# Gates from PSUM, spill experts behind the places, turned parts from ScalarE: one change to a two-layer attention and expert kernel

## What is computed

```python
# block 1: cross attention to ctx, 16 heads of 8
x = x + attention(ln(x), ctx, ctx) @ Wo.T + bo
# block 2: 8 experts of 128, two per token, and a shared one
logits = h @ gate_w.T                       # gate0
idx = top_k(logits + lb_bias, 2)
w = sigmoid(logits[idx]); w = w / (sum(w) + 1e-6)
x = x + sum_e w_e * (relu(h @ w1[e].T)**2 @ w2[e].T) + shared
# block 3: causal self attention (q1, k1, v1), norm, attention to ctx (k2, q2), norm,
#          c + relu(c @ Wf + bf), norm
# block 4: router (gate1), the first of the softmax's top two, 7 routed experts of 512, a shared one
probs = softmax(h @ w_router); top = argmax(probs)
x = x + 2 * probs[top] * (silu(h @ w_gate[top]) * (h @ w_up[top])) @ w_down[top] + shared
```

## Time and profile before

| | us |
|---|---|
| median of 3 runs | 356.95 (356.26 to 357.55) |
| the profiled execution | 356.45 |
| its span, first to last instruction | 354.4 |
| TensorE busy in it | 283.8 |
| VectorE busy | 279.7 |
| ScalarE busy | 205.7 |
| GpSimd busy | 156.7 |

### The profile page before, as it was taken

The page is one execution under the profiler, slowest core; times in us unless marked ns, Lnnn a source line. Parts: engine busy times, 40 slices in busy tenths (PEclk is TensorE's granted clock), DMA queues, the critical chain, the costliest instruction groups (busy, mean ns, idle before and its releaser), DMA issues.

```text
span 354.4 us, 8691 instructions
## 1 busy us (share of the span) xinstructions
PE 283.8 (80%) x3349; PEld 210.3 (59%) x3349; DVE 279.7 (79%) x726; ACT 205.7 (58%) x431; POOL 156.7 (44%) x157
## 2 busy tenths in 40 slices
PE   0396864549999977999997988574797999979994
PEld 0154653424566733787775866433564799758993
DVE  4889999796745589689899557878779998897732
ACT  1464873334757444898886689431873558735561
POOL 9904669653653030344544334411431567442541
PEclk9999995556999989999999899766679999999999
DMA  8502022432020000000000000000003102040030
GB/s 249 227 1 91 13 79 91 130 138 91 15 112 0 0 2 1 3 2 2 4 2 1 2 3 2 2 0 0 2 2 139 42 2 93 2 178 2 18 107 30
DMA packets 6592, 16.62 MB, mean 47 GB/s; under 512 B 660, under 2 KB 2968, under 8 KB 6552
## 3 DMA queue, kind: packets, MB, share of 16 engines
q1 hardware_dynamic: 6552, 16.08, 12.9%
HBM read 10.83 MB, written 0.52 MB: 32 GB/s over the span
## 4 chain that ended last, share of the span: by engine, by line
PE 42%; DVE 34%; ACT 9%; POOL 7%; issue 7%; POOLq 0%; DVEq 0%; ACTq 0%
DVE MX L1337 6%; PE ps L985 5%; PE ps L776 5%; PE ps L777 5%; PE ps L778 5%; DVE prl L636 4%; PE ps L837 2%; ACT pr L1117 2%; DVE stat L1292 2%; ACT prh L1121 2%; ACT lnx L1163 2%; DVE pr L1518 2%; PE ps L973 2%; PE ps L909 1%; PE ps L825 1%
## 5 line engine op out<-in xcount | busy, mean ns | idle before, releaser
L636 POOL TENSOR_TENSOR prl<-pr,prh 128x384 f16<-128x384 f32 (+1 forms) x48 | 49.9, 1042 | 73.9 <-ACT prh L1121 73.9
L1117 ACT ACTIVATE pr<-ps 128x384 f32<-128x384 f32 (+1 forms) x96 | 51.7, 538 | 21.9 <-DVE prl L636 8.9
L1337 DVE TENSOR_REDUCE MX<-ps 128x8 f32<-128x512 f32 (+2 forms) x80 | 52.0, 681 | 8.5 <-PE ps L861 4.1
L1121 ACT ACTIVATE prh<-ps 128x384 f16<-128x384 f32 (+1 forms) x96 | 51.7, 538 | 0.3 <-PE ps L778 0.2
L642 POOL TENSOR_TENSOR prl<-pr,prh 128x512 f16<-128x512 f32 x28 | 33.5, 1205 | 41.1 <-ACT prh L1156 41.1
L745 POOL TENSOR_TENSOR wl<-wraw,wh 128x512 f16<-128x512 f32 (+1 forms) x30 | 35.2, 1198 | 29.3 <-DVE wh L1221 29.2
L636 DVE TENSOR_TENSOR prl<-pr,prh 128x384 f16<-128x384 f32 (+1 forms) x48 | 33.4, 695 | 8.0 <-ACT prh L1121 7.8
L1156 ACT CAST prh<-pr 128x512 f16<-128x512 f32 x28 | 17.2, 618 | 15.0 <-DVE pr L1518 14.8
L837 PE MATMUL ps<-cst,lnx 128*128 128x128 f32 x64 | 15.2, 383 | 12.8 <-DVE lnx L1359 9.9
L1518 DVE TENSOR_TENSOR pr<-ps,hr 128x512 f32<-128x512 f32 x28 | 18.9, 683 | 8.2 <-ACT hr L1150 7.9
L776 PE MATMUL ps<-VSh,prh 128*128 128x9 f16 x192 | 20.5, 169 | 3.7 <-POOL prl L636 3.3
(11 more groups left out here) (256 smaller groups left out, 1058.4 us busy)
## 6 DMA issues: line engine op xcount, KB each, us to landing
wraw<-in_weights SPq DMA_DIRECT2D x8, 768.0 KB, 4.0
wraw<-wh SPq DMA_DIRECT2D x6, 384.0 KB, 2.6
wraw<-wl SPq DMA_DIRECT2D x6, 384.0 KB, 3.0
wraw<-in_weights SPq DMA_DIRECT2D x2, 576.0 KB, 7.3
rowb<-in_rows SPq DMA_DIRECT2D x1, 708.0 KB, 5.2
wd<-in_down SPq DMA_DIRECT2D x1, 576.0 KB, 7.4
X<-in_x SPq DMA_DIRECT2D x1, 512.0 KB, 5.2
picks<-in_spread SPq DMA_DIRECT2D x1, 512.0 KB, 6.0
```

Of the source, the lines that this page charges most:

```text
L636: return engine.tensor_tensor(prl[:, g, three, 0:width], pr[:, g, buffer[("scores",) + e[1:]], 0:width], prh[:, g, three, 0:width], ALU.su ...
L1117: nc.scalar.activation(pr[:, g, buffer[e], 0:width], src[:, 0:width], ACT.Exp, scale=SCALE[a]).then_inc(pr_ready, 1)
L1121: nc.scalar.activation(prh[:, g, buffer3[e[1:]], 0:width], src[:, 0:width], ACT.Exp, scale=SCALE[a]).then_inc(prh_ready, 1)
L1337: nc.vector.tensor_reduce(o, src[:].rearrange("p (h k) -> p h k", h=heads), AX_X, ALU.max).then_inc(max_read, 1)
```

## The change

It moves these pieces of work:

- `gate0`: no copy to `lg`. ScalarE's Exp reads the logits in PSUM; VectorE waits for it and then adds the bias straight from PSUM. `gate1`: the maximum and the subtraction read PSUM.
- `turn` of `x1` and `x3`: ScalarE makes both the f32 copy `tF` and, after it, the f16 part `tH` from PSUM; VectorE only subtracts, from PSUM. The gate's product waits for the first of the two (`turn_whole`).
- `v1` is a kind of step of its own: ScalarE writes the high part, VectorE subtracts.
- `rank` no longer has the four operations for the spill experts; a new step `spill` has them, in three, behind it, and SP waits for `spill`.
- `out_norm`: one product of 256 elements.
- `nat k0` waits for the context's low part alone, `vctx` for the duplicates.
- The planner has new costs, `GROUP_LEAD` 2.4 in place of 1.1, and new weights in `PRESSING`, so the order on every engine is laid anew.

```diff
-GROUP_LEAD = 1.1
+GROUP_LEAD = 2.4
...
-PRESSING = {'add0': 214, 'add1': -540, 'b3_add': -124, 'back': 211, ...}
+PRESSING = {'add0': 214, 'add1': -154, 'b3_add': 145, 'back': 592, ...}
...
+        chain([("spill", g)], gate, *[("spill", 0)] * g)
+        if g:
+            also(("rank", 1), ("spill", 0))
...
-                    sp.wait_ge(which_ready, nth[("rank", g)])
+                    sp.wait_ge(which_ready, nth[("spill", g)])
...
-                        pe.wait_ge(ctx_ready, 3)
+                        pe.wait_ge(ctx_ready, 1)
...
-                    pe.wait_ge(turn_first, nth[("turn", "x1" if l == 0 else "x3", g)])
-                    take(bank[e][0], (g0_lg, g1_lg)[l], n)
+                    pe.wait_ge(turn_whole, WHOLE["x1" if l == 0 else "x3", g])
+                    take(bank[e][0], (g0_lg, g1_sub)[l], n)
...
-                    dst = tF[:, g, :] if name in ("x1", "x3") else tH[:, g, TURN[name][1], :]
-                    nc.scalar.copy(dst, src[:]).then_inc(turn_first, 1)
+                    if name in ("x1", "x3"):
+                        nc.scalar.copy(tF[:, g, :], src[:]).then_inc(turn_whole, 1)
+                    nc.scalar.copy(tH[:, g, TURN[name][1], :], src[:]).then_inc(turn_high, 1)
+                elif kind == "v1":
+                    g = e[2]
+                    sc.wait_ge(v1_mm, n)
+                    sc.wait_ge(zeroed, 10)
+                    nc.scalar.copy(VS[0][:, g, :, :, 0:D], src[:].rearrange("p (t h d) -> p t h d", t=T, d=D)).then_inc(v1_high, 1)
...
-                    sc.wait_ge(g0_lg, n)
-                    nc.scalar.activation(ex[:], lg[:], ACT.Exp, scale=-1.0).then_inc(g0_exp, 1)
+                    sc.wait_ge(g0_mm, n)
+                    if n > 1:
+                        sc.wait_ge(g0_ready, n - 1)
+                    nc.scalar.activation(ex[:].rearrange("p t x -> p (t x)"), src[:, 0:8 * T], ACT.Exp,
+                                         scale=-1.0).then_inc(g0_exp, 1)
...
-                    dve.wait_ge(turn_first, n)
-                    whole = src[:]
-                    if name in ("x1", "x3"):
-                        whole = tF[:, g, :]
-                        link(nc.vector.tensor_copy(tH[:, g, slot, :], whole))
-                    nc.vector.tensor_tensor(tL[:, g, slot, :], whole, tH[:, g, slot, :], ALU.subtract).then_inc(turn_ready, 1)
+                    dve.wait_ge(turn_high, n)
+                    nc.vector.tensor_tensor(tL[:, g, slot, :], src[:], tH[:, g, slot, :], ALU.subtract).then_inc(turn_ready, 1)
...
-                    for q in range(2):
-                        ins = nc.vector.tensor_tensor(
-                            o_n[:, g, 2 * (b % 2) + q, :].rearrange("p (h d) -> p h d", d=D), v[:, q, :, 0:D],
-                            rec[:, q, :].unsqueeze(2).broadcast_to([P, H, D]), ALU.mult)
-                    ins.then_inc(o_ready, 1)
+                    q0 = 2 * (b % 2)
+                    nc.vector.tensor_tensor(o_n[:, g, q0:q0 + 2, :].rearrange("p q (h d) -> p q h d", d=D), v[:, :, :, 0:D],
+                                            rec[:].unsqueeze(3).broadcast_to([P, 2, H, D]), ALU.mult).then_inc(o_ready, 1)
...
-                    dve.wait_ge(g0_mm, n)
-                    nc.vector.tensor_copy(lg[:].rearrange("p t x -> p (t x)"), src[:, 0:8 * T]).then_inc(g0_lg, 1)
+                    lb = rowb[:, len(ROWS) * P:len(ROWS) * P + 8]
+                    dve.wait_ge(g0_exp, n)
+                    nc.vector.tensor_tensor(zz[:], src[:, 0:8 * T].rearrange("p (t x) -> p t x", t=T), lb.unsqueeze(1).broadcast_to([P, T, 8]),
+                                            ALU.add).then_inc(g0_lg, 1)
...
-                    nc.vector.tensor_tensor(cmp8[:, :, 0:7], first_spill[:, 1:8].unsqueeze(1).broadcast_to([P, 3, 7]),
-                                            consts("nth", 3).unsqueeze(2).broadcast_to([P, 3, 7]), ALU.is_le)
-                    nc.vector.tensor_reduce(ended[:], cmp8[:, :, 0:7], AX_X, ALU.add)
-                    link(nc.vector.tensor_scalar(ended[:], ended[:], float(ROUTED - 1), None, ALU.min))
-                    nc.vector.tensor_scalar(which[:, g, 0:3], ended[:], float(PIECE), None, ALU.mult).then_inc(which_ready, 1)
...
+                elif kind == "spill":
+                    g = e[1]
+                    link(nc.vector.tensor_tensor(cmp8[:, :, 0:7], first_spill[:, 1:8].unsqueeze(1).broadcast_to([P, 3, 7]),
+                                                 consts("nth", 3).unsqueeze(2).broadcast_to([P, 3, 7]), ALU.is_le))
+                    link(nc.vector.tensor_reduce(ended[:], cmp8[:, :, 0:7], AX_X, ALU.add))
+                    nc.vector.tensor_scalar(which[:, g, 0:3], ended[:], float(ROUTED - 1), float(PIECE), ALU.min,
+                                            ALU.mult).then_inc(which_ready, 1)
```

More of the change, by code:

```diff
@@ L54 @@
 ARRIVES = {"ctx": 4.5, ("split", 0): 5.5, "split": 14.0, ("ln_stats", "x0"): 8.0, "bo_add": 10.0, "kbs_zero": 7.0}
-PRESSING = {'add0': 214, 'add1': -540, 'b3_add': -124, 'back': 211, 'bias': 104, 'bo_add': -101, 'ctx': 136, 'down0': 130, 'down1': -346, 'downr': 1609, 'gate0': 359, 'gate1': 878, 'hi1': -17, 'kblocks': 1011, 'kbs_zero': -574, 'ln_center': 235, 'ln_norm': -42, 'ln_plain': 882, 'ln_pow': 694, 'ln_stats': 695, 'lo1': 990, 'masks0': -180, 'masks1': 13, 'max': 108, 'nat': 745, 'negmax': 1082, 'onehot': -128, 'onehot_t': -914, 'out_norm': 871, 'plow': 962, 'plow_pool': -340, 'pv': 253, 'rank': 1267, 'scores': 108, 'sort_high': -100, 'sort_low': 38, 'split': -31, 'split_low': -1573, 'spots': -649, 'spread': 1033, 'square': 744, 'stack': 121, 'turn': 682, 'up0': 150, 'up1': -357, 'vctx': 249, 'xsplit': -146}
+PRESSING = {'add0': 214, 'add1': -154, 'b3_add': 145, 'back': 592, 'bias': 180, 'bo_add': 251, 'ctx': -215, 'down0': 130, 'down1': -434, 'downr': 1609, 'gate0': 531, 'gate1': 922, 'hi1': -20, 'kblocks': 1211, 'kbs_zero': -580, 'ln_center': -7, 'ln_norm': -479, 'ln_plain': 998, 'ln_pow': 506, 'ln_stats': 695, 'lo1': 990, 'masks0': -180, 'masks1': 47, 'max': 108, 'nat': 752, 'negmax': 1062, 'onehot': -128, 'onehot_t': -961, 'out_norm': 1017, 'plow': 930, 'plow_pool': -340, 'pv': 773, 'rank': 1267, 'scores': 108, 'sort_high': -100, 'sort_low': 174, 'spill': 62, 'split': -31, 'split_low': -1511, 'spots': -350, 'spread': 1743, 'square': 745, 'stack': 123, 'turn': 682, 'up0': 146, 'up1': -674, 'v1': 600, 'vctx': 403, 'xsplit': -146}
 SHARED = 6
@@ L114, in attention @@
             if s[2] == 0:
-                also(("pv", *s), ("square", "v1", g) if a == 1 else ("vctx", a))
+                also(("pv", *s), ("v1", "v1", g) if a == 1 else ("vctx", a))
                 if s[1] % 2:
@@ L184, in steps @@
         also(("nat", "q1", g), ("nat", "k1", g))
-        chain([("square", "v1", g)], e)
+        chain([("v1", "v1", g)], e)
         e = attention(1, g, k, q)
@@ L278, in banks_of @@
         return 2
-    return int(e[0] in ("max", "scores", "up0", "ctx", "vctx", "nat", "stack", "turn", "square", "negmax", "gate0", "gate1",
+    return int(e[0] in ("max", "scores", "up0", "ctx", "vctx", "nat", "stack", "turn", "square", "v1", "negmax", "gate0", "gate1",
                         "spread", "rank", "sort_high", "sort_low", "spots", "downr"))
@@ L439, in build @@
                 nth_pv_before[e] = nth[("pv",) + scores[i - NPV][1:]]
+    whole = [e[1:] for e in orders["act"] if e[0] == "turn" and e[1] in ("x1", "x3")]
+    WHOLE = {e: i + 1 for i, e in enumerate(whole)}
     nth_split = [1 + 3 * i for i in range(PIECES)]
@@ L791, in _ @@
                     need_piece(WEIGHTS[f"v{e[1]}"][0])
+                    pe.wait_ge(ctx_ready, 3)
                     take(bank[e][0], vctx_ready, n)
@@ L843, in _ @@
                     pe.wait_ge(turn_ready, nth[("turn", {"v1": "x2", "f": "c"}.get(name, name), g)])
-                    take(bank[e][0], sq_read, n)
+                    take(bank[e][0], sq_read if kind == "square" else v1_read, n)
                     for t in range(T):
@@ L847, in _ @@
                         mm = split_mm(o[:, tt], (tH[:, g, slot, tt], tL[:, g, slot, tt]), weight(*WEIGHTS[name]))
-                    mm.then_inc(sq_mm, 1)
+                    mm.then_inc(sq_mm if kind == "square" else v1_mm, 1)
                 elif kind == "max":
```

43 lines of the change are left out of this document (20 added, 23 removed).

## The result

| | before | after |
|---|---|---|
| median of 20 runs each, us | 357.21 (353.39 to 360.41) | 360.41 (357.20 to 362.20) |
| ratio to before | | 1.0101 [1.0073, 1.0129] |
| profiled execution, its span, us | 356.45, 354.4 | 360.25, 358.2 |
| granted clock of TensorE, mean of the span | 0.906 | 0.890 |

The changed kernel is 1.0% slower, some 3.6 us: as much as I had forecast, on the other side, and outside the range of 349.5 to 358.5. Executions over 1.5% above their kernel's fastest are left out of all ratios; the trace under "One pair of steps" is of such an execution (361.26 us), as there is no other.

What follows compares the result with a forecast made beforehand. TensorE (80% busy) and VectorE (79%) limit by turns, stage by stage. Terms 0.8 + 0.4 + 1.2 + 0.6 + 0.3 + 0.7 - 0.4 = 3.6 us gave 352.85 profiled, 353.3 median; range 351 to 355.5, eight in ten 349.5 to 358.5.

Steps and rivals of the forecast that it cites:

- The order: Planner's new order on all four engines: costed at nothing, bounded by three misplaced steps either way, 4 us.
- slower: Rival: worse cover, group 1 entering its last normalisation 5 us later with group 0 done; about 358.3 us, chance 0.22.
- the two marks that I had named for a failure: Group 1's last x3 turned later than 299, or TensorE's idle time in 54 to 84 growing.
- gate0, group 0: Bias add from PSUM no longer waits for GpSimd, so the cast may finish an end earlier: 0.8 us, bounds 0 to 1.1.
- gate1 and places, group 1: Second gate loses a copy and hop (0.4 both groups together); places at 312.9 in place of 313.2.
- gate1 and places, group 0: Second gate loses a copy and hop (0.4 both groups together); spill operations leave the line to the places: 0.4.
- turned parts: x1 and x3 casts go to ScalarE, VectorE subtracts from PSUM: 1.2 us, bounds 0 and 2.3.
- v1: High part moves to ScalarE, group 1's copy running beside the subtraction ahead: 0.6 us, bounds 0 and 0.7.
- out_norm: One product per output in place of two, 0.42 against 0.49 us; about five of twelve count: 0.3.
- ScalarE's copies: Second ScalarE copy in the turns delays what ScalarE does next: charge of 0.4 us, bounds 0 and 2.4.
- the case that I had priced at up to 1.65: gate0's Exp standing behind a layer norm's four scalings, VectorE waiting: up to 1.65 us, counted as 0.
- Spill: Spill operations off the line to the places: 0.7 us together, bounds 0.3 and 2.2; later spill-weight DMAs cost 0.

Runs made afterwards that it cites:

- One pair of steps: All edits in the order of before, but one upward and one downward TensorE step moved from ahead of group 0's sorts to behind them: 360.31 us, 1.0073.
- the dummies: Idle TensorE products of 512 columns, results overwritten, 50 ahead of ten waits; in the changed kernel's own order 355.94 us, 0.9973.
- All three other whole lists: With the edits: the changed kernel's order (repeat 1.0067), its planner with GROUP_LEAD 1.1 (1.0136), and with old GROUP_LEAD and old PRESSING (1.0195).
- GROUP_LEAD put back: The changed kernel with GROUP_LEAD 1.1 in place of 2.4, weights and costs as after: 361.86 us, 1.0136.
- with the turned parts as before: All edits in the order of before, but x1 and x3 turned as in the kernel before: 357.75 us, 1.0016.
- dummy products in both: 50 dummy products added to the edits in the old order (351.50 us, 0.9846) and to the kernel before without edits (353.05 us, 0.9893).
- The edits in the old order: All edits of the changed kernel, each engine's steps pinned to the order of the kernel before: 356.22 us, 0.9982.
- the new order without the edits: The operations of the kernel before, none of the edits, in the changed kernel's order: 360.65 us, 1.0119.

## Why the prediction was wrong, step by step

**The order.** This is the first step that failed: the order was costed "at nothing", with a bound of 4 us. It was +3.0 us with the edits and +4.2 without, the very end of my bound. I bounded one misplaced step by its length and by the idle time it leaves. The pair of steps showed 3.2 us for one place (0.9982 to 1.0073), since a bare wait also costs the clock of what follows (0.57 in place of 1.00 in the 8 us around the sorts). That the clock is most of the loss from group 0's second gate on is shown by the dummies; what the loss ahead of it consists of (some 0.5%) stays open. Nor was nothing the likeliest value. All three other whole lists here are slower than the list of before.

**The rival that came true** was "slower", by another mechanism than I gave. I let group 1 enter its last normalisation 5 us later and pay at the density of 340 to 354. It did enter later (x3 turned at 301.9, not 299.4, one of the two marks that I had named for a failure), but from the sort to the end nothing was lost beyond 0.17 us, and GROUP_LEAD put back made it no better. That the direction was among my rivals was no insight into the mechanism.

**The terms of the sum** are the second step that failed: 3.6 us were forecast, 0.6 arrived. Measured in the old order:

| term | forecast, us | measured |
|---|---|---|
| gate0, group 0 | 0.8 | 0.2 |
| gate1 and places, group 1 | 0.2 and some 0.3 | 0.43 by the places' end, 0.16 at the sort (16.20, and 16.04 with the turned parts as before) |
| gate1 and places, group 0 | 0.2 and 0.4 | at most 0.2 (gate to sort 12.83, now 12.66) |
| turned parts | 1.2 | 0.9 at TensorE |
| v1 | 0.6 | 0.1 |
| out_norm | 0.3 | 0.0 to 0.1 |
| ScalarE's copies | -0.4 | in the 0.9 |
| all edits, whole kernel | 3.6 | 0.6 (0.9982), 1.7 with dummy products in both (0.9846 / 0.9893); give or take 1.3 and 1.9 |

**gate0.** The edits in the old order, VectorE around it, then TensorE:

```profile
71.99 0.18 DVE L1406 TENSOR_TENSOR zz<-ps,rowb 128x32 f32<-128x32 f32 x1
...
73.29 0.51 DVE L1415 CAST i8f<-i 128x32 f32<-128x32 uint32 x1
73.84 1.19 DVE L1417 TENSOR_TENSOR sel<-cst,i8f 128x32 f32<-128x32 f32 x2
...
76.76 0.19 DVE L1427 TENSOR_TENSOR wt<-zz,r 128x32 f32<-128x32 f32 x1
...
73.81 1.11 PE L850 MATMUL ps<-cst,lnx 128*128 128x128 f32 x4 [1.23 <-ACT lnx L1185]
77.73 2.07 PE L998 MATMUL ps<-wd,pr 128*128 128x128 f32 x8 [2.81 <-DVE pr L1521]
```

The add no longer waits (0.18), as I said, and the cast is down from 1.09 to 0.51. But the pair of comparisons behind it takes 1.19 in place of 0.29: it has met the GpSimd operation that the cast got past. From its first step to `wt` gate0 took 5.17 us before (copy included) and 4.96 now, and TensorE's wait for the first expert's product is 2.81 after 2.80. I had told this very mechanism for `jump`, that a wait "is not saved but handed on", and did not apply it two paragraphs earlier. The rule of the Trainium skill that I cited (SBUF — State Buffer, Who interferes with whom) agrees with both: the add with one operand in SBUF ran free, the next operation with two paid. What this stage gained lies ahead of x1's transposes of group 1, where TensorE's wait is 1.23 us above. In before it was 1.85:

```profile
74.82 1.11 PE L837 MATMUL ps<-cst,lnx 128*128 128x128 f32 x4 [1.85 <-ACT lnx L1163]
```

0.4 of that is the turned parts' (GpSimd's power, above), 0.2 are left for gate0: its Exp, which had run at 73.00 right ahead of the layer norm's scalings, no longer waits for VectorE's copy and runs at 71.32.

In the new order the wait that the change adds does come. ScalarE and VectorE of after:

```profile
73.44 1.65 ACT L1178 ACTIVATE lnx<-X,shift,rstd 128x128 f32<-128x128 f32 x4 [2.78 <-DVE shift L1312]
75.00 0.17 ACT L1139 ACTIVATE ex<-ps 128x32 f32<-128x32 f32 x1
...
75.20 0.19 DVE L1399 TENSOR_TENSOR zz<-ps,rowb 128x32 f32<-128x32 f32 x1 [1.79 <-ACT ex L1139]
```

The Exp stands behind a layer norm's scalings, and VectorE waits 1.79 us for it: the case that I had priced at up to 1.65 and then left out. It did not eat all of the gain: from x1's transposes of group 0 to the first expert's product it took 12.13 us there, 12.85 in the new order without the edits (10.07 and 10.67 in the old order). At the second gate of group 1 the same wait was 1.61. An added wait and a new order have to be weighed together.

**x3, second gate and places, group 1.** TensorE and VectorE of the edits in the old order:

```profile
300.50 1.01 PE L966 MATMUL ps<-wg,tF 128*128 128x8 f32 x8
311.72 0.62 PE L1090 MATMUL ps<-act,route 128*128 128x128 f16 x8
316.05 3.20 PE L1060 MATMUL ps<-route,lni 128*128 128x512 f16 x16 [0.43 <-DVE route L1486]
...
301.81 0.18 DVE L1433 TENSOR_REDUCE r<-ps 128x4 f32<-128x32 f32 x1
308.16 0.77 DVE L1463 SCALAR_TENSOR_TENSOR jump<-first_spill,cst 128x8 f32<-128x8 f32 x1
310.08 0.17 DVE L1472 CAST pos<-pos 128x4 f16<-128x4 f32 x1
310.28 0.18 DVE L1476 TENSOR_TENSOR cmp<-first_spill,cst 128x21 f32<-128x21 f32 x1
311.38 0.28 DVE L1506 TENSOR_TENSOR act<-ps,act 128x128 f16<-128x128 f32 x1
312.45 3.54 DVE L1486 TENSOR_SCALAR route<-copies,pos 128x1280 f16<-128x1280 f16 x4 [0.19 <-PE ps L1090]
```

VectorE reads the gate 1.31 us after its product starts (2.03 in the earlier trace rows), and the places end 8.44 us behind that read (8.87 before): 0.72 and 0.43, near the forecast of 1.0 and 0.5. But `route` starts 2.2 us behind the places and not 1.7. It waits for TensorE's last product on the old `route` (311.72), that product waits for `act` (311.38), and `act` stands on VectorE behind `spill`, whose three operations (310.28 to 310.88) now come right behind the places. So of 1.15 us the sort sees 0.65: taken out from ahead of the places, the work was still ahead of the sort. (Where `spill` stands is part of how the edits were put into the old order; in after one product comes first, and `route` starts 3.6 us behind the places.) That `onehot` waits for group 0's last product stood in my own description of the kernel, and I did not ask what is late next.

**v1.** ScalarE's copy, then VectorE's subtraction, then TensorE, same kernel:

```profile
134.48 0.59 ACT L1124 CAST VSh<-ps 128x512 f16<-128x512 f32 x1 [0.73 <-PE ps L790]
...
135.10 0.69 DVE L1383 TENSOR_TENSOR VSl<-ps,VSh 128x512 f16<-128x512 f32 x1 [0.54 <-ACT VSh L1124]
...
135.94 0.38 PE L838 MATMUL ps<-tH,picks 128*128 128x512 f16 x1 [0.64 <-DVE VSl L1383]
```

The copy starts only when the product is done, so it does not run beside what VectorE does ahead: VectorE idles 0.54 us for it. TensorE's wait went from 0.75 to 0.64. Moving half of a chain of two to another engine does not shorten the chain.

**out_norm.** 0.42 for 0.49, as worked out, but TensorE waited 9.9 us for it before and 9.8 with the edits in the old order, and o0's stage took 9.74 and 9.75 us. **Spill** and **k0** went as said: the DMAs of late `which` cost nothing, and k0's product, free to start earlier, waits for the bias (3.8 us in place of 1.5) until nearly the same time.

## What to carry to other kernels

An edit that gives the planner new costs is two changes, and the second may be the larger: pin the old order first and time the edits in it. A wait of an engine for the port, for another engine or for a bank is mostly handed on to the next in line, so a saving counts only from the place where it reaches the engine that ends the stage. And steps that fill TensorE's waits are worth more than their length here, as they also hold its clock; where nothing real is left to fill with, dummy products did it, but only where they stood ahead of a wait of the very order that they were put into.

## What the runs showed of the hardware

- **The clock as a price.** In 29 runs of the unchanged kernel beside the first experiments the time at 0.50, worked out from the mean granted clock as 2 x (1 - clock) x span, was 65 us with a spread of 6, and the span grew with it by 0.25 us for each us (correlation 0.92; in three later sets of 17 to 23 runs 0.17 to 0.26, correlation 0.73 to 0.89). So most of the scatter between runs of one kernel goes with the clock. The Trainium skill (TensorE: Matmul & The Clock Gate, Part 1) says that an idle TensorE is gated down to 1.2 GHz; the traces agree. It puts the warm-up at under 1% of a typical span; here, where the clock falls again and again, 50 dummy products brought 1.4%.
- **What one wait did.** With waits of 0.95 and 1.19 us in 269 to 271 the clock stayed at 1.00 in the sorts, with 1.83 more ahead of them it fell, and transposes and sorts took 9.31 us in place of 7.02.
- **PSUM reads of this size cost nothing extra.** The 128x32 steps that now read PSUM took 0.18 to 0.19 us, like those from SBUF, in all runs. The 0.3 us that the figure of the Trainium skill (VectorE: DVE Perf Modes, the TRN2 errata) would have added to the sum did not come.
- **The port conflict goes both ways.** GpSimd's 128x4 power took 1.47 us beside a VectorE operation with two SBUF operands and 1.14 beside one that reads PSUM (1.03 to 1.04 in most of its other places).
